# A fused attention and mixture-of-experts kernel: head 0's maxima inside the projections, merged score units masked by VectorE, token placing in the last head

## The chip, the cores and the metric

The kernel runs on one core of a Trainium2 chip. The metric is the device time of one execution in microseconds; lower is better. Three timed runs of the kernel before took 2096.61, 2099.18 and 2100.73 us, a median of 2099.18.

## The reference

Two branches read the same layer-normed input of B = 2 sequences, S = 2048 tokens, D = 512, in float32, and both are added to the input.

```python
xn = layernorm(x)                                   # [2, 2048, 512]
# attention: H = 16 heads of HD = 32, causal, with an ALiBi bias on the key position
q, k, v = (heads(xn @ W + b) for W, b in ...)
scores = einsum('bhqd,bhkd->bhqk', q, k) / sqrt(32) + slopes[h] * (key - (S - 1))
scores = where(causal, scores, finfo.min)
attn_out = softmax(scores) @ v -> merge heads -> @ Wo + bo
# experts: router on an RMS norm of xn, top 2 of E = 8, renormalised
topw, topi = top_k(softmax((norm_w * rms(xn)) @ router_w.T), 2)
a = silu(xn @ gate_w[e]) * (xn @ up_w[e]);  y = sum_e cw[e] * (a @ down_w[e]) * 4
out = x + attn_out + y
```

## The kernel before, in words

Each engine has its own in-order program; semaphores tie them. There are three stages, each a block at whose end all engines meet.

**Projections** (`project`, L200 to L700). Eight chunks of 512 tokens. A chunk has 12 PSUM tiles: four of q, four of k (by head columns) and four of v (by token rows), each the sum of 12 float32r matmuls of 512 columns (high and low parts). ACT rounds a tile (`qk_high`), DVE takes the remainder (`qk_low`), SP stores both to DRAM; v goes through DVE, ACT and POOL (`v_low`). The next chunk's input is normalised and transposed meanwhile. Router matmuls (`router_tiles`) stand at the end of a chunk, in the last chunk ahead of the v tiles. SP waits at the end until all stores have landed.

**Attention** (`attend`). 32 heads, one after another. A slot of three holds a head's `k_st` and `q_st` (rows of high and low parts, two bias rows, two rows for the query's maximum) and `v_split`. For each head there are
- M: 40 `maximum_tile` matmuls of the *next* head, up to 512 keys wide, whose row maxima DVE takes (`take_maximum`; the diagonal ones with a mask), then X (`fold_maxima`), W (`transpose_maxima`, `maxima_rows`) and a DMA that places the maxima as rows of the next head's `q_st`. The exponent then needs no subtraction;
- S: 40 score units (128 keys x up to 512 queries). On the diagonal a unit is narrower (512, 384, 256, 128 columns) and a second matmul, identity times a bf16 mask, is added (L1158). ACT takes the exponential (`weights`): unit kind P and Q twice (rounded, exact), kind W once;
- L: POOL's low part of kind P (L905); D: DVE's low part of kind Q (L981);
- V: `value_products`, two float32r matmuls for P and Q (L1170, L1172), one float32 matmul for W (L1176);
- O: ACT copies the sums, DVE adds, SP stores.

The letters of the string `ORDER` give the order in which every engine meets these (`BACK` says how many units V, L and O lag behind). `KIND` gives each unit's kind, `P_RING` the slots for probabilities. Before head 0, the attention stage loads slots 0 and 1, POOL fills the constant rows (`k_ones`, `q_ones`), DVE counts the tokens of each expert (`count_tokens`), all 40 maxima of head 0 are formed one after another, and then DVE places the tokens (`place_tokens`) ahead of its first work for head 0. The last head has no M units; in it DVE also inverts the first batch's weight sums (`first_inverses`, after the first O) and splits Wo (`split_wo`, after the second).

**Output and experts**: the output projection and 71 tiles of 128 token slots through their expert. POOL scatters the token lists first.

## Time and profile before

| | us |
|---|---|
| median of three timed runs | 2099.18 |
| the profiled execution | 2096.1 |
| its span, first to last instruction | 2094.3 |
| PE busy | 1988.7 |
| DVE, ACT, POOL busy | 1366.0, 1346.4, 1363.9 |
| granted TensorE clock, mean | 0.970 of 2.4 GHz |

Busy times are of one profiled execution. A matmul's row includes its way through the array, so consecutive rows overlap: the distance between two starts tells what one costs, not its length. "Idle before" is the engine's idle time ahead of a row and what ended it. A row that ends in x3 stands for three like it.

### The profile page before, as it was taken

The page shows a single profiled execution, that of the slowest core. Times are in us where ns is not written, and L with a number is a line of the kernel's source. Part 1 is how long each engine was busy: PE and PEld are TensorE (multiplying, and loading weights), DVE is VectorE, ACT ScalarE, POOL GpSimd, SP SyncE. Part 2 cuts the span into 40 slices and gives each one's busy share as a digit, 9 for nine tenths or more (in the row PEclk, how much of TensorE's full clock was granted, in tenths as well). Part 3 has the DMA queues.
Part 4 walks back from the last instruction along what each step waited for, and adds up shares of the span by engine and source line. Part 5 has one row for each costly group of instructions (what it writes and reads, how often), then busy time and mean ns, then how long its engine had stood idle before and what let it go on. Part 6 is the DMA issues. An engine that isn't in the chain of part 4 may idle for free. (4 is left out here: it accounts for less than half of the span.)

```text
span 2094.3 us, 40489 instructions
## 1 busy us (share of the span) xinstructions
PE 1988.7 (95%) x9182; PEld 1441.7 (69%) x9183; DVE 1366.0 (65%) x3106; ACT 1346.4 (64%) x2891; POOL 1363.9 (65%) x1262
## 2 busy tenths in 40 slices
PE   6999996799999999999999999999989989999996
PEld 4888885477777777777777777777746666666664
DVE  5454443888878888887878787888838843333332
ACT  4323321299999999999999999999972223333332
POOL 3110112188888888888989888888977625555554
PEclk9999998599999999999999999999999999999998
DMA  7577666423323232332324242323117755555554
GB/s 228 201 247 247 228 215 207 104 53 83 90 74 99 74 99 72 83 90 69 104 52 119 54 119 52 97 55 78 30 43 239 230 175 95 96 99 97 94 99 70
DMA packets 118487, 243.95 MB, mean 116 GB/s; under 512 B 15920, under 2 KB 52656, under 8 KB 112144
## 3 DMA queue, kind: packets, MB, share of 16 engines
q1 hardware_dynamic: 100464, 206.09, 33.8%
q0 software_dynamic: 17984, 37.38, 10.0%
q8 instruction: 19, 0.31, 0.1%
q14 instruction: 20, 0.16, 0.0%
HBM read 139.28 MB, written 104.21 MB: 116 GB/s over the span
## 5 line engine op out<-in xcount | busy, mean ns | idle before, releaser
L905 POOL TENSOR_TENSOR probs_lo<-probs,probs_hi 128x512 fp32r<-128x512 f32 (+2 forms) x864 | 1018.4, 1205 | 182.0 <-ACT probs L937 175.3
L936 ACT ACTIVATE probs_hi<-s_ps 128x512 fp32r<-128x512 f32 (+2 forms) x1024 | 642.5, 627 | 116.5 <-PE s_ps L1158 106.9
L937 ACT ACTIVATE probs<-s_ps 128x512 f32<-128x512 f32 (+3 forms) x1120 | 628.5, 586 | 4.7 <-PE s_ps L1155 1.1
L972 DVE TENSOR_REDUCE m_part<-m_ps 128x1 f32<-128x512 f32 x768 | 500.2, 685 | 59.3 <-PE m_ps L1137 58.0
L1155 PE MATMUL s_ps<-q_st,k_st 100*128 100x512 f32 (+1 forms) x880 | 330.2, 391 | 11.7 <-DVE probs_lo L981 5.2
L1137 PE MATMUL m_ps<-k_st,q_st 98*128 98x512 f32 (+2 forms) x880 | 325.3, 408 | 12.0 <-DVE m_part L969 6.6
L1170 PE MATMUL o_ps<-probs_hi,v_split 128*96 128x512 f32 x704 | 286.8, 407 | 0.1
L969 DVE CUSTOM_DVE_ANT_0 m_ps<-m_ps,mask_row 128x128 f32<-128x128 f32 (+3 forms) x512 | 250.8, 499 | 52.0 <-PE m_ps L1137 41.5
L1172 PE MATMUL o_ps<-probs_lo,v_split 128*96 128x512 f32 x704 | 265.9, 378 | 0.0
L1530 POOL DMA_INDIRECT out<-y,tile_rows x71 | 114.3, 1610 | 170.1 <-issue 97.9
L1155 PEld LDWEIGHTS s_ps<-q_st,k_st 100*128 100x128 f32 x880 | 168.1, 191 | 74.3 <-issue 18.0
L420 POOL TENSOR_TENSOR v_rows<-v_raw,v_rows 128x512 fp32r<-128x512 f32 x32 | 41.2, 1286 | 272.3 <-ACT v_rows L466 272.3
L1137 PEld LDWEIGHTS m_ps<-k_st,q_st 98*128 98x128 f32 x880 | 168.6, 196 | 70.7 <-DVE m_part L969 20.9
L1607 DVE SCALAR_TENSOR_TENSOR gated<-th,h_ps 128x256 f32<-128x256 f32 x71 | 29.9, 421 | 204.7 <-ACT th L1571 204.7
L1155 PE MATMUL s_ps<-q_last,k_last 100*128 100x512 f32 (+3 forms) x400 | 147.9, 385 | 0.0
L1137 PE MATMUL m_ps<-k_last,q_last 98*128 98x512 f32 (+3 forms) x400 | 143.1, 390 | 1.0 <-DVE m_part L969 0.3
L1571 ACT ACTIVATE th<-h_ps 128x256 f32<-128x256 f32 x71 | 27.3, 385 | 178.1 <-PE h_ps L1650 178.1
L981 DVE TENSOR_TENSOR probs_lo<-s_ps,probs_hi 128x512 fp32r<-128x512 f32 (+1 forms) x160 | 106.4, 665 | 53.5 <-ACT s_ps L937 52.3
L1667 PE MATMUL y_ps<-w_down,inner_t 128*128 x284 | 133.7, 593 | 0.7 <-issue 0.7
L996 DVE TENSOR_TENSOR high_sums<-o_ps,high_sums 32x512 f32<-32x512 f32 x128 | 87.7, 685 | 71.5 <-ACT high_sums L943 67.3
L1172 PEld LDWEIGHTS o_ps<-probs_lo,v_split 128*96 128x96 f32 x704 | 116.0, 165 | 21.1
L1170 PEld LDWEIGHTS o_ps<-probs_hi,v_split 128*96 128x96 f32 x704 | 118.6, 168 | 16.9 <-POOL probs_lo L905 0.7
(192 smaller groups left out, 3655.4 us busy)
## 6 DMA issues: line engine op xcount, KB each, us to landing
v_d<-v_rows SPq DMA_DIRECT2D x7, 3072.0 KB, 10.0
v_split<-v_d SPq DMA_DIRECT2D x22, 768.0 KB
k_st<-k_hi_d SPq DMA_DIRECT2D x44, 256.0 KB
q_st<-q_hi_d SPq DMA_DIRECT2D x44, 256.0 KB
xs<-in_x SPq DMA_DIRECT2D x8, 1024.0 KB, 6.8
xn_d<-xs SPq DMA_DIRECT2D x8, 1024.0 KB, 12.1
q_hi_d<-qk_hi SPq DMA_DIRECT2D x32, 256.0 KB, 7.2
q_lo_d<-qk_lo SPq DMA_DIRECT2D x32, 256.0 KB, 7.6
```

The lines of the kernel that those rows point to most:

```text
L905: nc.gpsimd.tensor_tensor(*low_operands(u), ALU.subtract).then_inc(lo_ready_pool, 1)
L936: nc.scalar.activation(probs_hi[:, u % P_RING, 0:w], scores, ACT.Exp, scale=SCALE)
L937: nc.scalar.activation(scores if KIND[u] == "Q" else probs[:, u % P_RING, 0:w], scores, ACT.Exp, scale=SCALE).then_inc(p_ready, 1)
L969: V.tensor_tensor_reduce(scores, scores, mask_row[:, M_WIDE - w:], 1.0, NEG, ALU.add, ALU.max, top).then_inc(m_taken, 1)
L972: V.tensor_reduce(top, scores, AX.X, ALU.max).then_inc(m_taken, 1)
L981: V.tensor_tensor(probs_lo[:, u % P_RING, 0:w], s_ps[:, S_BANK[u], CH - w:CH], probs_hi[:, u % P_RING, 0:w].bitcast(F32), ALU.subtract).th ...
L1137: nc.tensor.matmul(m_ps[:, m % M_BUFS, 0:w], q_st[r][0:ROW_MAX, qt * P:(qt + 1) * P], k_st[r][0:ROW_MAX, k0:k0 + w], start=True, stop=True ...
L1155: last = nc.tensor.matmul(s_ps[:, S_BANK[u], CH - w:CH], k_st[r][0:ROWS, kt * P:(kt + 1) * P], q_st[r][0:ROWS, q0:q0 + w], start=True, sto ...
L1170: nc.tensor.matmul(o_ps[0:VS, qc % 2, at], v_split[r][:, kt, :], probs_hi[:, place, 0:w], start=(kt == 0), stop=True, skip_group_check=True)
L1172: last = nc.tensor.matmul(o_ps[0:VS, qc % 2, at], v_split[r][:, kt, :], probs_lo[:, place, 0:w], start=False, stop=True, skip_group_check= ...
L1530: nc.gpsimd.indirect_dma_start(out=out, out_offset=bass.IndirectOffsetOnAxis(ap=rows[:, r:r + 1], axis=0), in_=y[:, p, :], in_offset=None, ...
L1667: last = nc.tensor.matmul(y_ps[:, p], inner_t[:, p, k], rhs, start=(k == 0), stop=(k == KF - 1))
```

## The change

1. **Head 0's maxima in the projections.** The attention buffers are allocated ahead of `project`, and the projections' own buffers are laid over others that are free then. SP issues `load_slot(0, 0)` ahead of chunk 6 (seven DMAs; it then waits for the bias store and for the ones rows) and `load_slot(1, 1)` in chunk 7 behind the first q tile's stores. POOL's memsets of the ones rows move into the projections, those of slots 1 and 2 into chunk 7. PE forms the 40 maxima within the last four tiles of chunk 6 (3, 3, 3, 2) and in chunk 7 (0, 3, 3, 3, 2, 3, 3, 3, 3, 3, 3, 0), each ahead of a group of four projection matmuls; DVE takes each tile's maxima ahead of its work on that tile. The transpose, the maxima rows and their DMA close the projections. In chunk 7 the router matmuls move ahead of the k tiles. The values of slots 0 and 1 are loaded at the start of the attention stage, with a semaphore of their own. The waits for the last stores move behind head 0.
2. **Score units merged.** Per pair of query chunks the 128- and 384-column diagonal units share a unit, and the two 256-column ones share another: 34 units instead of 40, nearly all 512 wide. A merged unit has two score matmuls, and two (W) or four (P, Q) value matmuls; exponential and low part are one instruction. Kinds go from 27 P, 8 W, 5 Q to 25 P, 5 W, 4 Q. There are new `KIND`, `ORDER` and `BACK` strings (V lags by 8), nine slots for probabilities instead of eight.
3. **The mask by VectorE.** The mask matmuls go. `mask_scores` adds the mask to the diagonal blocks in PSUM, one instruction for one or two blocks, ten a head; ACT waits for it (`s_masked`).
4. **Tokens in the last head.** `count_tokens` and `place_tokens` become one generator. In the last head DVE runs one piece of it at each of 29 turns where other heads have an M unit; the rest follows behind. ACT's exponential for the shares and PE's two counting products stand at turns 2 and 5. The expert weights' loads no longer wait for the tokens.

```diff
+    beside = ((0,) * 2 * G + (3, 3, 3, 2), (0, 3, 3, 3, 2) + (3,) * 6 + (0,))
...
+            def load_slot(n, r):
+                for p in range(QK_RING):
+                    sp.wait_ge(qk_stored[p], 32 + 32 * 2 * G // QK_RING * (NCH // B))
+                *rows, bias = slot_loads(t, n, r)
+                for dst, src in rows:
+                    sp.dma_start(dst, src).then_inc(st_loaded[r], 16)
+                sp.wait_ge(al_stored, 32)
+                sp.wait_ge(k_ones, r + 1)
+                sp.dma_start(*bias).then_inc(st_loaded[r], 16)
...
+            load_slot(0, 0)
             chunk(NCH - 2, 0, False)
             chunk(NCH - 1, 1, False, last=True)
+            sp.wait_ge(q_ones, 1)
+            sp.wait_ge(m_rows_ready, 1)
+            for dst, src in maxima_places(t, 0):
+                sp.dma_start(dst, src).then_inc(m_placed, 16)
...
+            pool.wait_ge(pj_ready, NJ * (NCH - 1) + 1)
+            for p in range(2):
+                pool.wait_ge(xn_stored[p], 16 * NCH // 2)
+            for r in range(1, HEADS_RING):
+                ones(r)
...
                 for n in range(3):
+                    for m in maxima[n:n + 1]:
+                        maximum_tile(m)
...
+        units += [whole(a, kt) for kt in range(TPC * a + 1)] + [[from_diagonal(a, 3, 0), from_diagonal(a, 1, P)], whole(b, 0)]
+        units += [[from_diagonal(a, 2, 0), from_diagonal(b, 2, CH // 2)]]
+        units += [whole(b, kt) for kt in range(1, TPC * b + 1)] + [[from_diagonal(b, 3, 0), from_diagonal(b, 1, P)]]
...
-                last = nc.tensor.matmul(s_ps[:, S_BANK[u], CH - w:CH], k_st[r][0:ROWS, kt * P:(kt + 1) * P],
-                                        q_st[r][0:ROWS, q0:q0 + w], start=True, stop=not diagonal)
-                if diagonal:
-                    last = nc.tensor.matmul(s_ps[:, S_BANK[u], CH - w:CH - w + P], ident_r, mask_s, start=False, stop=True)
+                for qc, kt, q0, w, at in S_UNITS[u]:
+                    last = nc.tensor.matmul(s_ps[:, S_BANK[u], at:at + w], k_st[r][0:ROWS, kt * P:(kt + 1) * P],
+                                            q_st[r][0:ROWS, q0:q0 + w], start=True, stop=True)
...
+            def mask_scores(n, u):
+                at = s_diagonals(u)
+                if not at:
+                    return
+                dve.wait_ge(s_ready, NS * n + u + 1)
+                if len(at) == 1:
+                    blocks = s_ps[:, S_BANK[u], at[0]:at[0] + P].unsqueeze(1)
+                else:
+                    blocks = s_ps[:, S_BANK[u], 0:2 * (at[1] - at[0])].rearrange("p (a c) -> p a c", a=2)[:, :, 0:P]
+                V.tensor_tensor(blocks, blocks, t["consts"][:, 2:3, :].to_broadcast([P, len(at), P]), ALU.add
+                                ).then_inc(s_masked, 1)
...
+                    if kind == "S":
+                        mask_scores(n, u)
...
+                    if pieces and i in FREE_TURNS:
+                        next(pieces, None)
...
+            pieces = place_tokens()
+            step_n(NH - 1, maxima=False, then=(first_inverses, split_wo), pieces=pieces)
+            for _ in pieces:
+                pass
```

## Rows read from the trace of the kernel before

**Rows 1.** The page, part 1: busy time of each engine, share, instructions.
```profile
PE 1988.7 (95%) x9182; PEld 1441.7 (69%) x9183; DVE 1366.0 (65%) x3106; ACT 1346.4 (64%) x2891; POOL 1363.9 (65%) x1262
```
**Rows 2.** Busy time by stretch: length, engines with instruction counts, clock, DMA, GB/s.
```profile
0.00:347.00 347.00, 326.45 (x1536) 269.00 (x1537) 163.48 (x487) 110.28 (x211) 59.08 (x43) 0.96 0.67 224
347.00:396.70 49.70, 23.82 (x47) 12.59 (x46) 35.51 (x90) 2.14 (x3) 10.31 (x7) 0.55 0.58 152
396.70:438.00 41.30, 35.04 (x146) 25.22 (x147) 34.44 (x87) 29.61 (x65) 27.25 (x23) 0.79 0.24 60
438.00:1521.00 1083.00, 1078.45 (x5311) 776.18 (x5309) 882.51 (x2041) 1014.65 (x2281) 951.55 (x811) 1.00 0.31 79
1521.00:1567.00 46.00, 39.99 (x170) 24.39 (x168) 18.14 (x20) 38.44 (x88) 39.64 (x32) 0.93 0.16 48
```
**Rows 3.** Transposes of maxima, one a head: ns min/median/max, first and last start.
```profile
L1142 PE MATMUL m_ps<-consts,m_max x3: 272/273/382, 392.5 to 474.1; 128*16 128x128 f32 x3
...
L1142 PE MATMUL m_ps<-consts,m_max x2: 273/273/273, 1485.0 to 1520.9; 128*16 128x128 f32 x2
```
**Rows 4.** Timeline (start, us, engine, line) and DMA issues of the seam.
```profile
344.38 5.85 SPq L354 DMA_DIRECT2D v_d<-v_rows  x2
v_d<-v_rows SPq DMA_DIRECT2D x2, 1536.0 KB, 6.3
356.88 0.36 SPq L798 DMA_DIRECT2D pairs<-in_token_pairs  x1
...
393.58 1.55 SPq L819 DMA_DIRECT2D q_st<-m_rows  x2
...
396.68 0.77 PE L1155 MATMUL s_ps<-q_st,k_st 100*128 100x512 f32 x1 [3.82 <-DMA q_st<-m_rows]
...
404.12 0.18 DVE L1070 CAST add_after<-opens 1x72 int32<-1x72 f32 x1
...
404.70 1.37 PE L1137 MATMUL m_ps<-k_st,q_st 98*128 98x512 f32 x3 [6.26 <-DVE m_part L969]
```
**Rows 5.** Timeline of PE in two places of a running head.
```profile
1517.83 1.02 PE L1176 MATMUL o_ps<-probs,v_split 128*96 128x512 f32 x2
...
1518.92 0.39 PE L1155 MATMUL s_ps<-q_st,k_st 100*128 100x512 f32 x1
...
1521.98 0.40 PE L1155 MATMUL s_ps<-q_st,k_st 100*128 100x512 f32 x1
1522.22 0.23 PE L1158 MATMUL s_ps<-mask_r 128*128 128x128 bf16 x1
1522.26 0.45 PE L1170 MATMUL o_ps<-probs_hi,v_split 128*96 128x512 f32 x1
1522.55 0.39 PE L1172 MATMUL o_ps<-probs_lo,v_split 128*96 128x512 f32 x1
```
**Rows 6.** Groups by shape, 438 to 1521 (busy us, mean ns), and ACT's timeline.
```profile
L905 POOL TENSOR_TENSOR probs_lo<-probs,probs_hi 128x512 fp32r<-128x512 f32 x631 | 802.3, 1293 | 86.5 <-ACT probs L937 80.2
L969 DVE CUSTOM_DVE_ANT_0 m_ps<-m_ps,mask_row 128x256 f32<-128x256 f32 x120 | 51.6, 430 | 4.9 <-PE m_ps L1137 0.3
L969 DVE CUSTOM_DVE_ANT_0 m_ps<-m_ps,mask_row 128x128 f32<-128x128 f32 x120 | 35.3, 294 | 8.5 <-PE m_ps L1137 6.2
...
1537.38 0.69 ACT L937 ACTIVATE probs<-s_ps 128x512 f32<-128x512 f32 x1
1537.86 0.69 ACT L936 ACTIVATE probs_hi<-s_ps 128x512 fp32r<-128x512 f32 x1
```
**Rows 7.** Timeline: POOL and DVE side by side in two places, and PE after them.
```profile
398.88 1.26 POOL L905 TENSOR_TENSOR probs_lo<-probs,probs_hi 128x512 fp32r<-128x512 f32 x1 [33.06 <-ACT probs L937]
398.96 1.23 DVE L1048 CAST idx_f<-slot_tile_i 128x64 f32<-128x64 int32 x1
...
1536.21 9.58 POOL L905 TENSOR_TENSOR probs_lo<-probs,probs_hi 128x512 fp32r<-128x512 f32 x5 [0.32 <-ACT probs L937]
...
1544.19 1.65 PE L1155 MATMUL s_ps<-q_st,k_st 100*128 100x512 f32 x3 [4.83 <-DVE probs_lo L981]
```

More of the change, by code:

```diff
@@ L124 @@
 ATTEND = attend_order()
+FREE_TURNS = [i for i, (kind, u, back) in enumerate(ATTEND) if kind == "M" and "O" in [a[0] for a in ATTEND[:i]]]
 LOOPS = (NH - 2) // HEADS_RING
@@ L137, in bank_before, with units_between @@
     return (at, 0) if at is not None else (max(v for v in range(NS) if S_BANK[v] == S_BANK[u]), 1)
+def units_between(u):
+    return next(d for d in range(1, NS + 1) if P_SLOT[(u - d) % NS] == P_SLOT[u])
+PV_START = max(units_between(u) for u in range(NS))
 VS = 3 * HD
@@ L311, in project @@
         v_low_ready = sem(ctx, "v_low_ready")
-        v_stored = [sem(ctx, f"v_stored{p}") for p in range(2)]
         al_loaded = sem(ctx, "al_loaded")
@@ L677, in _, with chunk @@
                 transpose_x(0, 0, k)
-            def chunk(c, par, ahead, last=False):
+            def chunk(c, par, ahead, last=False, first_maxima=((),) * NJ):
                 pe.wait_ge(xl_ready, 2 + KD * (c + 1))
@@ L1035, in place_tokens @@
-                step(V.tensor_tensor(starts[:, :], ends[:, :], padded[:, :], ALU.subtract))
-                step(V.tensor_tensor(base[:, :, :], so_far[:, :, :], counts[:, 1], ALU.subtract))
-                step(V.tensor_tensor(base[:, :, :], base[:, :, :], counts[:, 0], ALU.add))
-                step(V.tensor_tensor(base[:, :, :], base[:, :, :], starts[:, :].unsqueeze(1).to_broadcast([P, TT, E]), ALU.add))
+                step.issue(last)
+                yield
+                step.settle()
@@ new lines, in place_tokens @@
+                step.issue(V.tensor_tensor_scan(ends[:, :], t["ones"][:, 0:E], padded[:, :], 0.0, ALU.mult, ALU.add))
+                yield
+                step.settle()
+                step.issue(V.tensor_tensor(starts[:, :], ends[:, :], padded[:, :], ALU.subtract))
+                yield
+                step.settle()
+                step.issue(V.tensor_tensor(base[:, :, :], so_far[:, :, :], counts[:, 1], ALU.subtract))
+                yield
+                step.settle()
+                step.issue(V.tensor_tensor(base[:, :, :], base[:, :, :], counts[:, 0], ALU.add))
@@ L1039, in place_tokens @@
+                yield
+                step.settle()
+                step.issue(V.tensor_tensor(base[:, :, :], base[:, :, :], starts[:, :].unsqueeze(1).to_broadcast([P, TT, E]), ALU.add))
+                yield
+                step.settle()
                 for k in range(TOP_K):
                     last = V.tensor_tensor(hot[:, k], hot[:, k], base[:, :, :], ALU.mult)
-                step(last)
+                step.issue(last)
+                yield
+                step.settle()
                 for k in range(TOP_K):
@@ L1079, in _ @@
-            fold_maxima(0)
-            maxima_rows(0, False)
-            place_tokens()
-            def step_n(n, maxima=True, before=True, then=()):
-                for kind, u, back in ATTEND:
+                step.issue(V.tensor_scalar(after[:, :], firsts, float(P), 0.0, ALU.subtract, ALU.max))
+                yield
+                step.settle()
+                step.issue(V.tensor_tensor(opens[:, :], opens[:, :], past[:, :], ALU.max))
+                yield
+                step.settle()
@@ L1085, in step_n @@
+                yield
+                step.settle()
+                V.tensor_copy(after[:, :], opens[:, :])
+            def step_n(n, maxima=True, before=True, then=(), pieces=None):
+                for i, (kind, u, back) in enumerate(ATTEND):
                     if back and not before:
                         continue
+                    if kind == "S":
+                        mask_scores(n, u)
                     if kind == "O":
@@ L1178, in value_products @@
-                last.then_inc(pv_done, 1)
-            pe.sem_inc(pv_done, P_RING)
-            pe.wait_ge(hot_ready, 1)
-            hot2 = both[:, :, :].rearrange("p t e -> p (t e)")
-            nc.tensor.matmul(o_ps[:, 1, 0:TT * E], t["triu"], hot2, start=True, stop=True)
-            nc.tensor.matmul(o_ps[:, 1, TT * E:2 * TT * E], t["ones"], hot2, start=True, stop=True).then_inc(counted, 1)
-            pe.wait_ge(st_loaded[0], 16 * ST_DMAS)
-            pe.wait_ge(q_ones, 1)
-            for m in range(NM):
-                maximum_tile(0, 0, m, first=True)
@@ L1198, in step_n @@
                     pe.wait_ge(st_loaded[r1], 16 * ST_DMAS * st_round)
-                for kind, u, back in ATTEND:
+                for i, (kind, u, back) in enumerate(ATTEND):
+                    if not maxima and i == FREE_TURNS[5]:
+                        count_tokens()
                     if kind == "S":
```

562 lines of the change are left out of this document (343 added, 219 removed).

## Prediction

> **What bounds the kernel now.** I read the engine line of the page first: TensorE (PE) is busy 95% of the span, the other engines 64 to 65% [rows 1]. The table of busy time by stretch then splits the span [rows 2]: projections 0 to 347 us, a seam 347 to 396.7, head 0 up to its transpose of maxima at about 438, thirty heads 438 to 1521, the last head 1521 to 1567, output and experts after that. In the thirty heads PE is busy 1078.45 of 1083.00 us, ScalarE (ACT) 94%, GpSimd (POOL) 88%, VectorE (DVE) 81%: PE sets the pace, and the period is (1520.9 - 474.1)/29 = 36.10 us a head [rows 3]. In the seam PE is busy 23.8 of 49.7 us at a granted clock of 0.55. In the last head PE has 6 us without work and ACT and POOL are what runs. Nothing in the output stage is touched, so its 527 us stay.
>
> **Scale.** The profiled execution took 2096.1 us (span 2094.3), the median of the three timed runs is 2099.18. The sum is made against 2096.1, and 3.1 us are added at the end.
>
> **1. The seam.** PE's last projection ends at 347.1; the first score matmul starts at 396.68, 49.6 us later. In between lie the store of the last values (issued by 350, 6.3 us to landing), the end of the block at 356.88 when SP issues its first load, the loads of slot 0, the token counts, 40 maxima one after another and the rows' DMA [rows 4]. The change puts slot 0's and slot 1's loads and all 40 maxima of head 0 inside projection chunks 6 and 7.
> - Added to the projections: 17,408 columns of maxima. A 512-column matmul holds the next one off for 0.235 us (0.24 from 1521.98 to 1522.22 [rows 5]), so 17,408/512 x 0.235 = 8.0 us on PE, which was already 100% busy there apart from the start. DVE has room: at most three maxima and one qk_lo, 512 wide, so about 0.7 us each by the slope of [rows 6] (0.136 us per 128 columns), 2.8 us in a tile of 15 matmuls, 3.5 us.
> - Left after the projections end (call it T): values of the last tile and their low part on POOL, to T + 2.7; then SP issues the last 1.5 MB store, and behind it the two maxima rows. They are on one queue, and the store takes 6.3 us to land [rows 4], so T + 9; the rows add what they took before, 396.68 - 395.13 (last issue) = 1.6 at most and less if they only queue. I take T + 9.7 for the first score matmul. Bounds: T + 6 if the rows overtake the store (issue ends at T + 4.3), T + 14 if the block change or slot 1 is late.
> - So 49.6 - 8.0 - 9.7 = **31.9 us saved** (27 to 36).
> The added DMAs on SP's queue: seven for slot 0 ahead of chunk 6's stores, with a new wait for the bias store to land; seven for slot 1 behind chunk 7's first stores, with a wait for POOL's memsets. Together 3.1 MB. Slot 0's 1.55 MB stand ahead of chunk 6's q and k stores and delay them by about 5 us (1.5 MB land in 6.3 [rows 4]); ACT, then DVE, wait on them, but four PSUM banks of 12 x 0.235 = 2.8 us each cover 11 us, so PE sees nothing of it in my sum. With that cover gone it costs up to 5 us in each of the two chunks. The first values now load after the block change, about T + 13; DVE needs 7 us for the 11 maxima that stand ahead of the first value product, so T + 16.7 is when they are wanted.
>
> **2. Head 0.** The stretch from its first score to its transpose took 41.3 us, more than a whole period of 36.1, though no value products of an earlier head are in it. In it PE waits 6.26 us for a maximum that DVE takes only after placing the tokens [rows 4], and its granted clock is 0.79 in the mean [rows 2]. Token placing leaves this place; the clock still starts at 1.2 GHz after PE's idle stretch. I take the wait and nothing more: **6 us saved** (3 to 8).
>
> **3. The period of a head, 31 times.** Removed: 16 mask matmuls a head (bf16, 128 columns). From a 512-wide score matmul over its mask to the second product behind it are 1522.55 - 1521.98 = 0.57 us, where two 512-wide matmuls alone take 0.47: a mask costs 0.10 us [rows 5], 16 x 0.10 = 1.6 us. Score and value pieces keep their count (a merged unit still has two matmuls for scores). The kinds change: columns through the two-product form fall from 30,208 to 29,696 (-0.23 us), columns of W units rise from 2304 to 2560; a W unit of 512 costs 1518.92 - 1517.83 - 0.235 (one other matmul between them) = 0.855 us [rows 5], so +0.43. Net 1.4 us: 34.7.
> Do the others follow? ACT: 72 exponentials with 32,512 columns become 63 with 32,256. A 512-wide one follows the last by 0.48 us [rows 6], so 63 and the four copies of sums make 67 x 0.48 = 32.2 us. POOL: 27 units of mixed width become 25 of 512 at 1.293 us [rows 6], 32.3 us. DVE: busy 882.51/30 = 29.4 us a head; one 384-wide Q unit less (-0.57 by the slope); ten mask additions, four of 128 and six of 256 columns. No such addition is in the trace; the nearest rows are the masked maxima of the same widths, 0.294 and 0.430 us [rows 6], which gives 3.8 us. Its hidden bound is 0 (in DVE's idle fifth), its exposed bound is under rivals. DVE comes to 32.6 us. So all three stay under 34.7, but at 93% each where they had 81 to 94% of a longer period. For that tightness I give back 0.15 us: 34.85, a gain of 1.25 x 31 = **38.8 us saved** (0 to 50).
>
> **4. The last head.** Here the 49 small DVE instructions of counting and placing tokens arrive, in 33 pieces over 29 turns. The 39 that place took 10.9 us in the seam, from about 393.4 to 404.30 [rows 4]; at that rate all take 14, and DVE has room on paper: 18 us busy of 46 [rows 2]. But POOL is busy 39.6 of 46 there, and the rows show the two holding each other up. A cast of 64 columns took 1.23 us and ended within 0.1 us of the POOL instruction that had started just ahead of it; five 512-wide POOL subtractions took 9.58 us instead of 6.4 while DVE split Wo, and PE then waits 4.83 us for DVE [rows 7]. If each of 33 pieces waits half a POOL instruction, 0.86 x 0.65 = 0.56 us, DVE gets 14 + 18 us more, and POOL, waiting for them in turn, some 11. POOL then has about 32 + 7 + 11 = 50 us of work against a head of 46. Minus 1.5 us for ACT's shorter list, plus the masks that wait behind pieces: **6 us lost** (gain 2, loss 25).
> The Trainium skill (SBUF - State Buffer, "Who interferes with whom") says why: a VectorE instruction with two SBUF inputs, or a copy or cast in a two-port mode, and a GpSimd instruction that reads SBUF exclude each other for their whole length, while one with a single SBUF input does not. By this rule the new masks (PSUM plus one SBUF operand) are free of it and the tokens are not; a sum without it would put the last head at -1.5 us. In both places of rows 7 the trace agrees with it.
>
> **Sum.** -31.9 - 6 - 38.8 + 6 = -70.7: 2096.1 - 70.7 = 2025.4, plus 3.1: **2028 us**.
>
> **Rivals.**
> - *Tokens and POOL lock fully.* Every blockable DVE instruction, about 44, waits 0.56 us and those inside a piece a whole one: the last head grows by 25 us instead of 6. 2028 + 19 = 2047. For: the two rows of the lock. Against: pieces are spread over turns at which DVE is otherwise idle. 15%. The page of the Trainium skill named above, taken at its word for every such instruction, is this case.
> - *The masks eat what TensorE gives.* A mask stands in DVE's in-order queue behind a reduction of 0.7 us and in front of ACT. If ACT, at 93%, waits for it, the period returns to 36.1 and part 3 is lost: 2028 + 38.8 = 2067. For: DVE loses most of its slack, and ACT's own is 2.6 us a head. Against: three score banks give a unit about 2 us from its matmul to its exponential, and score, mask and handovers need about 1.5. 12%.
> - *Slower than before.* The same mask fully exposed: 0.43 for the instruction, 0.35 for the one in progress, 0.2 for two handovers, about 1 us x 10 = 10 us on ACT's 32.2, a period of 42 us, 31 x 6 = 186 us lost against 33 to 38 won at the seam: 2099 + 150 = 2249. It becomes slower than before from a period of 37.2, that is from half of the masks exposed; ACT's own list allows 2.6 us of waiting before anything is lost. 5%.
> - *The maxima are not hidden.* Stores behind slot loads stall PE in both chunks: +10, 2038, inside the range. Part of the forecast's 68%.
>
> **Numbers.** Forecast (own range 2014 to 2040) 68%, tokens 15%, masks even 12%, slower 5%. The 80% range takes in the token case and the low end of parts 1 and 3: 2010 to 2055. A measurement of this kernel tells 0.2%, some 4 us, from no change. Faster 94%, same 1%, slower 5%.
>
> **What would show it.** First score matmul at about 365 us (355 + 9.7), released by the DMA of the maxima rows; no PE wait in chunks 6 and 7; a period of 34.7 to 35.0 us between transposes of maxima; mask additions of 0.29 and 0.43 us on DVE with ACT rarely released by them; a last head of 50 to 54 us with small DVE instructions lasting over 1 us. Wrong if the period is above 35.5, if PE stands idle in the projections, or if the last head is shorter than 46.

## The result, and the profile after

The changed kernel took 2080.48 us (median of 4 runs, 2078.02 to 2083.59) where the kernel before took 2099.31 (2096.61 to 2100.73): a ratio of 0.9915, 95% interval 0.9902 to 0.9929. That is faster by 18.8 us, or 0.9%. The forecast was 2028, range 2010 to 2055: the sign was right, three quarters of the gain did not come. The profiled execution has a span of 2076.2 us.

The stretches, cut at the same events as before (end of the last projection matmul, first score matmul, transposes of maxima, first product of the output stage), from the two traces:

| stretch | before | after | change | forecast |
|---|---|---|---|---|
| projections | 347.1 | 360.8 | +13.7 | +8.0 |
| seam | 49.6 | 9.1 | -40.5 | -39.9 |
| head 0 to its transpose | 41.0 | 30.7 | -10.3 | -7.3 |
| thirty heads | 1083.2 | 1087.8 | +4.6 | -37.5 |
| last head | 49.7 | 61.4 | +11.7 | +6.0 |
| output, experts | 523.7 | 526.4 | +2.7 | 0 |

By this table the change is -18.1 us where -70.7 was forecast; 42.1 of the missing 52.6 us are in the thirty heads.

The rows behind it: the page's engine line, the busy times by stretch, and the transposes of maxima, which now run from 400.6 to 1488.4. Thirty periods between them are 36.26 us each; before it was 36.11 over the same thirty.

```profile
PE 1954.8 (94%) x8670; PEld 1418.8 (68%) x8671; DVE 1442.9 (69%) x3391; ACT 1320.5 (64%) x2603; POOL 1360.5 (66%) x1199
```
```profile
0.00:360.80 360.80, 332.27 (x1576) 275.42 (x1577) 189.40 (x544) 110.19 (x211) 69.94 (x49) 0.96 0.69 225
360.80:369.90 9.10, 0.29 (x2) 0.09 (x1) 1.41 (x4) 1.91 (x2) 1.31 (x2) 0.63 0.85 263
369.90:400.60 30.70, 30.70 (x130) 22.69 (x131) 28.46 (x70) 26.92 (x55) 25.17 (x20) 0.89 0.49 131
400.60:1488.40 1087.80, 1062.21 (x4832) 757.95 (x4831) 948.77 (x2310) 991.06 (x2011) 946.25 (x752) 1.00 0.31 79
1488.40:1549.80 61.40, 41.54 (x158) 25.81 (x157) 43.49 (x80) 39.85 (x81) 42.07 (x31) 0.90 0.13 38
...
L1374 PE MATMUL m_ps<-consts,m_max x31: 276/277/278, 400.6 to 1488.4; 128*16 128x128 f32 x31
```

In the fourth line against its partner in [rows 2] the reader sees what failed: TensorE has 479 matmuls less in thirty heads (16 masks each) and is busy 16.2 us less, but the stretch is not shorter. TensorE stands idle 25.6 us in it, where it stood 4.6 us before. It no longer sets the pace alone. (A matmul that is held back can still count as busy; the experiments below come back to this.)

The seam went as forecast. Its timeline answers to [rows 4]: the last two value stores are issued between 357.45 and 363.95, the two rows of maxima behind them from 364.06 on, and they release the first score matmul at 369.90.

```profile
357.45 6.50 SPq L454 DMA_DIRECT2D v_d<-v_rows  x2
...
364.06 3.25 SPq L510 DMA_DIRECT2D q_st<-m_rows  x2
...
369.90 0.80 PE L1385 MATMUL s_ps<-q_st,k_st 100*128 100x512 f32 x1 [7.87 <-DMA q_st<-m_rows]
```

The waits of the running heads (420 to 1500; engine, line, what it waited for, us in total, times, longest). Two are new, against none of their kind in the kernel before: ScalarE waits for VectorE's masks (the third row, 71.6 us, or 2.4 us a head), and it waits for a DMA that empties `high_sums` (the last row, 0.7 us a head). PEld is TensorE's loading of weights, which overlaps its matmuls.

```profile
POOL probs_lo L1061 <- ACT probs L1092: 140.0, 205, 1.5
PEld s_ps L1385 <- ACT probs L1092: 74.6, 176, 1.5
ACT probs_hi L1091 <- DVE s_ps L1155: 71.6, 60, 1.5
...
ACT high_sums L1098 <- DMA weight_sums_d<-high_sums: 20.2, 25, 1.4
```

The masks cost VectorE about what the forecast (0.430 and 0.294) took from the masked maxima of the same widths, 0.441 and 0.292 us (groups by shape, 400.6 to 1488.4):

```profile
L1155 DVE TENSOR_TENSOR s_ps<-s_ps,consts 128x256 f32<-128x256 f32 x180 | 79.3, 441 | 1.6
...
L1155 DVE TENSOR_TENSOR s_ps<-s_ps,consts 128x128 f32<-128x128 f32 x120 | 35.0, 292 | 0.9
```

In the last head the tokens' pieces and the split of Wo meet POOL. Timeline of 1511 to 1524: six POOL subtractions take 11.42 us, where at the running heads' 1.29 us each they would take 7.7, pieces of 8 columns take 1.2 us each, and TensorE waits 7.95 us for a low part that stands behind all of it.

```profile
1511.29 11.42 POOL L1061 TENSOR_TENSOR probs_lo<-probs,probs_hi 128x512 fp32r<-128x512 f32 x6 [1.30 <-ACT probs L1092]
```
```profile
1515.92 3.24 DVE L1351 TENSOR_TENSOR wo_lo<-wo_raw,wo_hi 128x2048 fp32r<-128x2048 f32 x1
1519.08 1.22 DVE L1219 TENSOR_SCALAR padded_i<-so_far 128x8 int32<-128x8 f32 x1
1520.34 1.18 DVE L1222 TENSOR_SCALAR padded_i<-padded_i 128x8 int32<-128x8 int32 x1
...
1523.19 0.69 DVE L1142 TENSOR_TENSOR probs_lo<-s_ps,probs_hi 128x512 fp32r<-128x512 f32 x1
```
```profile
1523.93 0.79 PE L1385 MATMUL s_ps<-q_st,k_st 100*128 100x512 f32 x1 [7.95 <-DVE probs_lo L1142]
```

### The profile page after: what moved, and what is told of

Its sections match the earlier page's. It is cut to its first block and busy times, and to the rows that moved or that the text cites. A ratio compares the mean times of both kernels' runs of the same rounds, so it can differ in the third digit from the quotient of the medians.

```text
span 2076.2 us, 38386 instructions
## 1 busy us (share of the span) xinstructions
PE 1954.8 (94%) x8670; PEld 1418.8 (68%) x8671; DVE 1442.9 (69%) x3391; ACT 1320.5 (64%) x2603; POOL 1360.5 (66%) x1199
## 3 DMA queue, kind: packets, MB, share of 16 engines
q0 software_dynamic: 17984, 37.38, 10.3%
## 5 line engine op out<-in xcount | busy, mean ns | idle before, releaser
L1061 POOL TENSOR_TENSOR probs_lo<-probs,probs_hi 128x512 fp32r<-128x512 f32 x800 | 1013.5, 1296 | 168.3 <-ACT probs L1092 168.0
L1091 ACT ACTIVATE probs_hi<-s_ps 128x512 fp32r<-128x512 f32 x928 | 597.4, 644 | 93.7 <-DVE s_ps L1155 91.2
L1092 ACT ACTIVATE probs<-s_ps 128x512 f32<-128x512 f32 x960 | 595.5, 651 | 0.2 <-DVE s_ps L1155 0.2
L1134 DVE TENSOR_REDUCE m_part<-m_ps 128x1 f32<-128x512 f32 x744 | 490.7, 684 | 11.3 <-PE m_ps L1369 5.6
L1385 PE MATMUL s_ps<-q_st,k_st 100*128 100x512 f32 (+3 forms) x880 | 323.6, 409 | 35.2 <-ACT probs L1092 17.1
L1369 PE MATMUL m_ps<-k_st,q_st 98*128 98x512 f32 (+2 forms) x840 | 281.7, 377 | 0.0
L1403 PE MATMUL o_ps<-probs_hi,v_split 128*96 128x512 f32 (+3 forms) x748 | 279.0, 383 | 1.0 <-POOL probs_lo L1061 0.5
L1404 PE MATMUL o_ps<-probs_lo,v_split 128*96 128x512 f32 (+3 forms) x748 | 269.9, 364 | 0.0
L1131 DVE CUSTOM_DVE_ANT_0 m_ps<-m_ps,mask_row 128x128 f32<-128x128 f32 x496 | 241.6, 497 | 19.2 <-PE m_ps L1369 12.8
L1404 PEld LDWEIGHTS o_ps<-probs_lo,v_split 128*96 128x96 f32 x748 | 122.9, 164 | 39.9 <-issue 6.4
L594 ACT ACTIVATE qk_hi<-pj,b_col 128x512 fp32r<-128x512 f32 x64 | 43.8, 686 | 139.4 <-PE pj L831 102.9
L1155 DVE TENSOR_TENSOR s_ps<-s_ps,consts 128x256 f32<-128x256 f32 (+1 forms) x320 | 116.2, 381 | 14.4 <-PE s_ps L1385 11.8
## 6 DMA issues: line engine op xcount, KB each, us to landing
xn_d<-xs SPq DMA_DIRECT2D x8, 1024.0 KB, 11.4
```

Source lines behind the costliest of these rows:

```text
L1061: nc.gpsimd.tensor_tensor(*low_operands(u), ALU.subtract).then_inc(lo_ready_pool, 1)
L1091: nc.scalar.activation(probs_hi[:, P_SLOT[u]], scores, ACT.Exp, scale=SCALE)
L1092: nc.scalar.activation(scores if KIND[u] == "Q" else probs[:, P_SLOT[u]], scores, ACT.Exp, scale=SCALE).then_inc(p_ready, 1)
L1131: V.tensor_tensor_reduce(scores, scores, mask_row[:, M_WIDE - w:], 1.0, NEG, ALU.add, ALU.max, top).then_inc(m_taken, 1)
L1134: V.tensor_reduce(top, scores, AX.X, ALU.max).then_inc(m_taken, 1)
L1155: V.tensor_tensor(blocks, blocks, t["consts"][:, 2:3, :].to_broadcast([P, len(at), P]), ALU.add).then_inc(s_masked, 1)
```

## The experiments

There are sixteen runs in four groups of four. "Period" is the distance of the first and last transpose of maxima in running heads, divided by 30. A ratio is against the kernel before on the same chip, with its 95% interval. The first group's chip was slower in the output stage (576 to 583 us there, at a granted clock of 0.92 to 0.93, against 522 to 528 at 0.97 elsewhere), with the kernel before at 2149.4 us. Its whole times are read only as ratios. Its periods are compared directly with those of the other groups, because the granted clock in the thirty heads is 1.00 on both chips (0.97 in e2 alone); no kernel was profiled on both. Every run that leaves the masks out has the exponent's scale at an eighth.

### Who pays for the masks?

First the masks are left out, to see whether ScalarE's 2.4 us of waiting is the loss.

```
-                if s_diagonals(u):
-                    act.wait_ge(s_masked, masked_count(n, u))
-                else:
-                    act.wait_ge(s_ready, NS * n + u + 1)
+                act.wait_ge(s_ready, NS * n + u + 1)
...
+                return          # mask_scores, VectorE
```

> The changed kernel without its masks: VectorE adds none and ScalarE waits for TensorE's score alone (the causal mask of the scores is left out, and the exponent's scale is an eighth so that nothing overflows; instructions and shapes are otherwise the same). The changed kernel has a period of 36.26 us a head where 34.85 was forecast, and in it ScalarE waits 2.4 us a head for masks. Theory A, the masks on VectorE hold the period, by the wait or by their 3.8 us of work a head: the period falls to 34.6 to 35.0, the time to 2033 to 2045. Rival B, the new order with its merged units is bound elsewhere (VectorE and ScalarE waiting for each other over the maxima and sums): the period stays at 36.0 to 36.3, the time at 2073 to 2081.

2130.66 us, ratio 0.991 (0.9894 to 0.9927); period 36.22. Theory A fell: without any mask the new order is no faster. ScalarE's idle time a head is 3.3 us, where the changed kernel had 3.2; it now waits 2.1 us for TensorE where it had waited for a mask.

```profile
L1370 PE MATMUL m_ps<-consts,m_max x31: 276/277/278, 401.5 to 1488.0; 128*16 128x128 f32 x31
```

The second run was to part ScalarE's wait from VectorE's work, with a sum of constants in the masks' place:

```
-                V.tensor_tensor(blocks, blocks, t["consts"]..., ALU.add)
+                V.tensor_tensor(masked[:, 0:w], cols, cols, ALU.add)   # w = 256 or 384
```

> The changed kernel in which VectorE, at the place of each mask, still waits for the score and then adds two stretches of a constant tile of 256 or 384 columns into a spare one (about as long as the mask it stands for), but ScalarE waits for the score alone (the mask is left out of the scores, the exponent's scale is an eighth). Tells A apart in two. A1, the wait of ScalarE for the mask is what costs: as without masks, period 34.7 to 35.1, time 2035 to 2048. A2, VectorE's added time is what costs: the period stays at 35.9 to 36.3, time 2070 to 2081. Rival B expects 36.0 to 36.3 here too, and in the run without masks.

2337.2 us, ratio 1.0853 (1.0821 to 1.0886), period (1700.7 - 412.5)/30 = 42.9. No theory had this, and the run says nothing of A1 or A2, because the stand-in was not like the mask. Both its operands and its result are in SBUF, and it took 1130 ns in the mean, where the masks, on PSUM, took 292 and 441.

```profile
L1153 DVE TENSOR_TENSOR masked<-consts 128x384 f32<-128x384 f32 (+1 forms) x320 | 361.5, 1130 | 18.7 <-PE s_ps L1382 16.1
```

Then the masks went back to TensorE, in the new order:

```
+                    if masked:
+                        last = nc.tensor.matmul(s_ps[:, S_BANK[u], at:at + P], t["ident_r"], t["mask_s"], start=False, stop=True)
```

> The changed kernel with its masks added by TensorE again, one matmul for each of the 13 diagonal blocks of 10 units (in the kernel before it was 16 blocks); merged units and order as changed. By the sum of what TensorE issues, some 34.2 us a head and 13 masks of 0.06 to 0.09: 35.0 to 35.4. Theory A: the period is 35.1 to 35.6, the time 2047 to 2062, faster than the changed kernel. Rival B: TensorE wasn't what bound it, the period stays at 36.2 to 36.6, the time at 2079 to 2092.

2168.95 us, ratio 1.0093 (1.0076 to 1.0109); period 37.27. (The expectation's "13 diagonal blocks" is miscounted: ten units hold 16.) It is worse than both theories allow. Against e1, sixteen masks cost 1.05 us a head, 0.066 each, so TensorE's work is still on the path of the new order; and with its masks where they were, the new order and its merged units are 1.16 us a head slower than the old. The fourth run is the old order with VectorE's masks:

```
+                    dve.wait_ge(s_ready, NS * n + u + 1)
+                    V.tensor_tensor(block, block, t["consts"][:, 2, :], ALU.add).then_inc(s_masked, 1)
```

> The kernel before with one edit: its 16 masks of a head are added by VectorE (at 0.29 us each, 4.6 us a head) at the place of the score in VectorE's order, and ScalarE waits for them. TensorE is rid of 16 matmuls, about 1.0 us of a period of 36.10. Theory A (a mask behind VectorE's queue holds ScalarE): 16 waits instead of 10 cost more than TensorE gives, period 37 to 39, time 2125 to 2185. Rival B (the masks are nearly free on VectorE): 35.1 to 36.0, time 2069 to 2096.

2274.19 us, ratio 1.0563 (1.053 to 1.0595); period (1640.2 - 440.8)/30 = 39.98. Here a mask behind VectorE's queue does hold ScalarE, and TensorE behind it: +4.4 us against the old order without masks (35.54, below). ScalarE waits for masks 124 us in 26 heads, 4.7 us a head (450 to 1500):

```profile
ACT probs_hi L951 <- DVE s_ps L1004: 72.8, 89, 2.4
...
ACT probs L952 <- DVE s_ps L1004: 51.2, 80, 1.1
```

So the mechanism of the forecast's rival is real. Something in the changed kernel keeps it out: its ten masks instead of 16 (the merged units), its order, or both; no run parts them.

### Where the 1.25 us went

The changed kernel was run again, for times on the chip of this group.

> The changed kernel as it is, for times on the same chip as the edits of this group. Its period was 36.26 us a head in the profile; here 36.2 to 36.3, and against the kernel before a ratio of 0.990 to 0.993, as measured.

2083.0 us, ratio 0.9926 (0.9907 to 0.9945), period 36.27.

> The kernel before without its 16 mask matmuls a head (the causal mask of the scores is left out, the exponent's scale an eighth so that nothing overflows); the order and its 40 units are as before. In its trace TensorE goes on 54 ns after each mask, 0.86 us a head, and its period is 36.10. Theory G, in the old order the masks' time comes back in full: period 35.0 to 35.3, so that the new order and units without any mask (36.22) lose about 1.1 us a head by themselves. Rival H, the old order too is held by the round with ScalarE: the period stays at 35.8 to 36.1, and nothing was to be had by taking the masks off TensorE.

2076.56 us, ratio 0.9907 (0.9886 to 0.9928); period 35.54. The period lies between the theories: of the 1.6 us that the forecast took away for 16 masks, the old order gives 0.57.

```profile
L1142 PE MATMUL m_ps<-consts,m_max x31: 272/273/273, 437.3 to 1503.4; 128*16 128x128 f32 x31
```

The two traces tell why, by the distances from one matmul's start to the next. In the kernel before, a mask has 0.054 us to the next start, 0.86 us a head, and the products of high parts take 0.53 us a head more than in e7 (7.79 and 7.26); 360 of the 480 masks in thirty heads have such a product right behind them. Together this is 1.39 us for 16 masks. Of these the period gains 0.57; the other 0.82 us come back at other matmuls: a 128-wide score now has 0.17 us to the next start, where it had 0.07. TensorE's idle time hardly shows it (5.7 us in thirty heads, 4.6 before), but its weight loads do. They now wait for ScalarE and VectorE 40.7 us where they waited 11.4, about 1 us a head more (438 to 1503; first the kernel before, then e7):

```profile
PEld s_ps L1155 <- DVE probs_lo L981: 7.0, 29, 0.2
...
PEld s_ps L1155 <- ACT probs L937: 4.4, 26, 0.2
```
```profile
PEld s_ps L1155 <- DVE probs_lo L981: 20.7, 60, 0.5
PEld s_ps L1155 <- ACT probs L937: 20.0, 69, 0.5
```

The new DMA wait was tried by moving the store that it waits for. In the changed kernel SyncE issues, each head, eight loads and then the store of the last sums (timeline of SyncE's queue):

```profile
1284.76 0.34 SPq L969 DMA_DIRECT2D k_st<-k_hi_d  x1
...
1287.78 0.35 SPq L963 DMA_DIRECT2D v_split<-v_d  x1
1288.17 0.43 SPq L981 DMA_DIRECT2D ctx_d<-high_sums  x1
1288.64 0.28 SPq L982 DMA_DIRECT2D weight_sums_d<-high_sums  x1
```

```
                 sums = 0
+                if before:
+                    store_context(n - 1, QCS - 1)
+                    sums += 1
                 if load_ahead:
...
-                    if kind == "O" and (before or not back):
+                    if kind == "O" and not back:
```

> One edit of the changed kernel: in each head SyncE issues the context and weight-sum stores of the head before (chunk 3) ahead of the eight loads for two heads on, not behind them. In the changed kernel ScalarE waits some 0.77 us a head, ending in DMA weight_sums_d, before it takes the sums of chunk 1 into the buffer that this store empties, and 1 us later TensorE waits 0.57 us for ScalarE. Theory C, this store behind the loads is one of the things that ate the gain: both waits go, the period falls to 35.5 to 35.9, the time by 10 to 22 us. Rival D, the wait is slack of the round between TensorE and ScalarE and another comes in its place: the period stays at 36.1 to 36.3.

2062.56 us, ratio 0.9834 (0.9817 to 0.9852), 20.4 us below the changed kernel on the same chip; period 35.61. Theory C holds. ScalarE's sums no longer wait for any DMA, and the waits of TensorE's weight loads for ScalarE fall from 74.6 to 47.2 us, TensorE's idle time in the thirty heads from 25.6 to 15.4:

```profile
POOL probs_lo L1064 <- ACT probs L1095: 119.3, 178, 1.4
ACT probs_hi L1094 <- DVE s_ps L1158: 72.4, 58, 1.6
PEld s_ps L1388 <- ACT probs L1095: 47.2, 123, 1.0
```

With the store out of the way, the masks were left out once more.

> The changed kernel with its stores first and without masks (the causal mask of the scores is left out, the exponent's scale an eighth). Period with stores first alone: 35.61. Theory K, the masks on VectorE are free in this order, store or no store: 35.5 to 35.65, which is the 35.54 of the old order without masks, so that order and merged units gave nothing by themselves. Rival L, their cost was only hidden under the wait for the store: 34.7 to 35.3.

2055.45 us, ratio 0.9782 (0.9758 to 0.9806); period 35.51. Theory K holds: ten masks on VectorE cost 0.10 us a head together, and the new order without them is as fast as the old order without them (35.51 and 35.54).

### What holds the rest

Five units a head (kind W) are multiplied in fp32. In the next two runs they are multiplied as two fp32r products instead, both of the rounded probabilities, so that the low part of these units is left out: first with the stores where they were, then with the stores first.

```
-                        last = nc.tensor.matmul(dst, values.bitcast(F32), probs[here], ...)
+                        nc.tensor.matmul(dst, values, probs_hi[here], ...)
+                        last = nc.tensor.matmul(dst, values, probs_hi[here], start=False, ...)
```

> The changed kernel with the five units a head that are multiplied as fp32 (kind W) multiplied instead by two fp32r products of their rounded probabilities (the products of these units are then not the reference's; ScalarE's work is the same, POOL's and VectorE's too). In the traces an fp32 unit of 512 columns is followed by 0.6 us more of TensorE than two fp32r products of 512, and the changed kernel has four of 512 and one of 384 where the kernel before had three of 512, one of 256 and four of 128. Theory E, the fp32 units are on the path and their new choice is part of the loss: the period falls by 0.8 or more, to 34.0 to 35.4. Rival F, ScalarE sets the period (it is busy 33.0 us of 36.26): what TensorE saves shows as waits of TensorE, the period stays at 35.9 to 36.3.

2064.71 us, ratio 0.9836 (0.9811 to 0.9861), period 35.64: a gain of 0.63, less than theory E's 0.8, but F is out.

> The changed kernel with its stores first and its five fp32 units a head multiplied as two fp32r products of their rounded probabilities (their products are then not the reference's). With the stores behind the loads this edit gave 0.63 us a head, and the stores first alone gave 0.66. Theory P, TensorE's own work and the holds between it and ScalarE set the period, and the two gains add: 34.8 to 35.1. Rival Q, ScalarE with 33 us of work sets it once the store is out of the way: 35.4 to 35.6.

2038.78 us, ratio 0.9714 (0.9696 to 0.9733), period (1448.8 - 404.4)/30 = 34.81. Theory P holds: the gains add (0.79 here), and TensorE's own work is on the path. Then ScalarE was relieved instead. From head 1 on, its second exponential of 26 of the 34 units covers 256 columns instead of 512, and the rest of the columns keep what an earlier unit left:

```
+                w = CH if isinstance(n, int) or KIND[u] == "Q" or S_UNITS[u][0][1] == 0 else CH // 2
```

> The changed kernel with its stores first, in which ScalarE's second exponential of 26 of the 34 units a head covers 256 columns instead of 512 from head 1 on (the rest of these columns stays what an earlier unit left there; the exponent's scale is an eighth in all units). In the kernel before such an instruction took 449 ns for 256 columns and 654 for 512, so ScalarE has some 5.3 us a head less. Rival Q, ScalarE sets the period: it falls by 2 us or more, to 31 to 33.6, or to where POOL's 31.5 us of low parts bind. Theory P, TensorE does: 34.6 to 35.5, with TensorE's waits for ScalarE (45.7 us in the loops in stores first alone) mostly gone.

2055.89 us, ratio 0.9797 (0.9781 to 0.9813), period 35.33. ScalarE is busy 4.3 us a head less (28.8 instead of 33.1), and the period falls by 0.28. The run does not clear ScalarE quite: it now waited for masks more often, 168 times in 28 heads where stores first alone had 57 in 29:

```profile
ACT probs_hi L1094 <- DVE s_ps L1159: 129.8, 168, 2.0
...
PEld s_ps L1389 <- ACT probs L1096: 17.8, 28, 0.6
```

The last run of this part moves a place in the ring of banks. The scores of 34 units go round three banks of PSUM, so twice a head a bank is taken again after two units instead of three, by units 33 and 1; here this is rotated to units 1 and 3:

```
-S_BANK = [u % S_BUFS for u in range(NS - 1)] + [1]
+S_BANK = [([v % S_BUFS for v in range(NS - 1)] + [1])[(u - 2) % NS] for u in range(NS)]
```

> The changed kernel with its stores first and the banks of the scores rotated by two units: 34 units go round 3 banks, so one bank is taken again after two units instead of three, twice a head; as it stands unit 33 waits for unit 31's exponentials there (TensorE stands 0.64 us in every head before its first product), rotated it is units 1 and 3. Theory R, this stand is on the path: it goes and nothing of its size takes its place, the period falls to 34.9 to 35.3. Rival S, ScalarE was busy then, and its next wait for TensorE (1.3 us before unit 1) grows or TensorE waits one unit on: 35.5 to 35.8.

2087.5 us, ratio 0.9946 (0.9929 to 0.9963), period (1498.6 - 405.3)/30 = 36.44. Both theories were wrong: TensorE's idle time at the old place shrank by only 0.27 us (0.48 to 0.21), and 7 us later, before unit 3, it loses 0.83 us. The old place of the short distance was the better one.

### Last head and first stage

All four runs of this part have their stores first and are read against e5. In the last head the split of Wo was moved behind the last sum:

```
-            step_n(NH - 1, maxima=False, then=(first_inverses, split_wo), pieces=pieces)
+            step_n(NH - 1, maxima=False, then=(first_inverses,), pieces=pieces)
...
             add_sums(NH - 1, QCS - 1)
+            split_wo()
```

> The changed kernel with its stores first (the edit of the run before) and a second edit: in the last head VectorE splits Wo (spread_r, wo_hi, wo_lo, some 6 us, with POOL's product beside it stretched from 7.7 to 11.4 us over six) after its last piece of the tokens and the last sum, not between them after chunk 0. From the last head's transposing row to the first product of the output stage it is 62.1 us with stores first alone, 49.7 in the kernel before. Theory I, the split in the middle holds ScalarE and TensorE behind VectorE (waits of 7.3 and 7.9 us): 54 to 58 us, the whole 3 to 8 us less than stores first alone. Rival J, the pieces themselves are the price, or the split now is late for the output: 61 to 65 us, no gain or a loss of up to 3 us.

2057.63 us, ratio 0.981 (0.9794 to 0.9827). The stretch is 57.6 us instead of 62.1; the last value product comes 51.6 us after the transpose instead of 58.1. Theory I holds. Alone, the split takes VectorE 3.9 us instead of 6.2:

```profile
1526.09 0.40 DVE L1349 CAST spread_r<-spread_raw 64x512 fp32r<-64x512 f32 x1
1526.60 1.23 DVE L1352 CAST wo_hi<-wo_raw 128x2048 fp32r<-128x2048 f32 x1
1527.86 2.29 DVE L1354 TENSOR_TENSOR wo_lo<-wo_raw,wo_hi 128x2048 fp32r<-128x2048 f32 x1
```

Then all token pieces were put behind the head, with the split left in its middle:

```
-            step_n(NH - 1, share_at=FREE_TURNS[2])
+            step_n(NH - 1)
             take_sums(NH - 1, QCS - 1)
+            share_weights()
```

> The changed kernel with its stores first, and all of the assignment of tokens (VectorE's pieces, ScalarE's share, TensorE's count) after the last head's work instead of in its free turns; the split of Wo stays where it was. Theory J, the pieces in the free turns are the price of the last head: its heads' work ends 8 to 12 us earlier than in stores first alone, but the tokens then stand alone behind it, some 15 to 20 us of short VectorE instructions, so the last stretch is 65 to 72 us and the whole 3 to 10 us slower. Theory I, the split of Wo is the price: the last head's own work ends no more than 4 us earlier, the last stretch is 72 to 80 us, the whole 10 to 18 us slower.

2064.79 us, ratio 0.9841 (0.9825 to 0.9858). The last value product comes at 48.3 us (9.8 sooner), the output stage at 64.7 (2.6 later). So the pieces cost 9.8 us in the head and the split 6.5, not independently. Put behind the head, the pieces lengthen the way from the last product to the output stage from 4.0 to 16.4 us, 12.4 more, so by the profiled runs the free turns are still their better place; the whole times (0.9841 and 0.9834) don't tell the two apart.

In the first stage the loads of slot 0 were issued inside chunk 6:

```
-            load_slot(0, 0)
-            chunk(NCH - 2, 0, False)
+            chunk(NCH - 2, 0, False, slot=True)      # load_slot(0, 0) after the stores of g == G
```

> The changed kernel with its stores first, and SyncE issues the loads of slot 0 after the fifth tile's stores of the projections' chunk 6 instead of ahead of the chunk. In the traces ScalarE waits up to 7.2 us there for a store of q (DMA q_lo_d) that stands behind these loads, and TensorE waits 2.8 to 4.9 us for VectorE's x_lo that comes of it; the projections ended 13.7 to 21 us later than in the kernel before, where 8.0 were forecast. Theory M, the loads ahead of the chunk's stores make this wait: it goes or falls under 1 us, the projections end 3 to 7 us sooner than with stores first alone (367.7). Rival N, the loads are only moved to where they delay other stores, or come late for the first maxima: no change within 1.5 us, or up to 5 us later.

2063.35 us, ratio 0.9839 (0.982 to 0.9859); the projections end at 361.5, within the 360.2 to 368.1 that this point takes over the changed kernel and its edits. The wait for x_lo (2.8 us in the changed kernel, 1.6 to 4.9 in the others) is gone, and another has its place, as rival N had it. Slot 0's loads now come late for the first maxima:

```profile
PE mp L816 <- DMA k_st<-bias_d: 4.2, 1, 4.2
```

> The changed kernel with its stores first, the split of Wo after the last head's sums, and the loads of slot 0 issued after the third tile's stores of chunk 6 (neither ahead of the chunk, where TensorE then waited 2.8 to 4.9 us for VectorE's x_lo, nor after the fifth's, where it waited 4.2 us for DMA k_st from bias_d instead). Theory M, this place is between the two waits: the projections end at 356 to 360 and the whole is 3 to 6 us below the run with stores first and late split (2057.6). Rival N: either wait comes back in another size, 361 to 365, the whole within 2 us of it.

2055.31 us, ratio 0.9792 (0.9772 to 0.9812); projections to 364.9, and the wait for the bias row is 3.0 us. Rival N holds. Against e8's ratio of 0.981 this is no measurable step. With stores first and the late split, it has the lowest time of the kernels here that leave nothing of the computation out: 2.1% below the kernel before, 1.2% below the changed one by the ratios (0.9792/0.9915).

## Why the prediction was wrong, point by point

- **Part 1: the seam right, its price in the projections too small.** The first score came at T + 9.1 where T + 9.7 was said, released by the maxima rows. The 8.0 us added to the projections were 13.7 in the profiled run, and more in others (364.5 in after_again against 347.7 in e7, the old order on the same chip: 16.8). So the part saved 26.8 us where 31.9 were said. The forecast said that four banks of PSUM would cover the stores behind slot 0's loads. They did not: ScalarE waited 7.2 us for a store of q (DMA q_lo_d) behind the loads (4.6 at the longest before, when TensorE did not wait), VectorE 6.98 for ScalarE, and TensorE 2.8 us for x_lo in chunk 6; two waits of 0.9 us for maxima came on top. e11 and e14 show that this wait comes from the place of the loads, and that each other place tried has a wait of its own. The maxima rival (+10) was right in mechanism, at a little over half its size (5.7).
- **Part 2, head 0: right, a little small.** The stretch took 30.7 us, 10.3 less, where 6 and 1.25 were said. TensorE's wait of 6.3 us is gone (it is busy 30.70 of 30.70 us), as forecast. The rest came with 16 matmuls fewer and a granted clock of 0.89 instead of 0.79, for which the forecast took nothing; no run parts the two.
- **Part 3, the period: wrong; this is the step that failed.** The forecast was 34.85, the period 36.26. The runs give one chain of steps to it:

```
36.11  kernel before
-0.57  its 16 masks left out (e7): 35.54; the forecast took 1.6
-0.03  new order, merged units, new kinds, stores first, no masks (e10): 35.51; the forecast took +0.20
+0.10  ten masks on VectorE (e5): 35.61; the forecast took +0.15 for tightness
+0.66  the last sums' store behind eight loads (after_again): 36.27; not in the forecast
```

  The chain depends on its order: in the new order, stores behind the loads, the same 16 masks on TensorE are worth 1.05 us and not 0.57 (e1, e3). No run has the new order with stores first and masks on TensorE, so how much is the mask's price and how much the order's is not settled between the two.

  Two steps of the forecast failed. First, a mask's 0.10 us was read at one place and multiplied by 16, as if TensorE's time came back whole. Over thirty heads 16 masks took 1.39 us, 0.087 each, so the price was a little high; the greater error is that only 0.57 of it came back, because TensorE then waits for ScalarE and VectorE (e7). "Busy 99.6%" said that TensorE was hardly ever seen idle. It did not say how far away the next wait was. Second, the forecast followed the changed instructions of four engines but not the new distance between a store that did not change and its reader: in one late head the store of weight_sums_d is issued 16.3 us after the transpose (15.1 before), and the sums that need its buffer are wanted at 22.8 us (in the same head of e5; 25.95 before): 6.5 us between them where there had been 10.8, and ScalarE stood until 23.8. The question "Do the others follow?" was asked of the engines' busy time alone. That busy time itself was forecast well: ScalarE 33.0, VectorE 31.6 and GpSimd 31.5 us a head, where 32.2, 32.6 and 32.3 were said.
- **The rival "masks eat what TensorE gives" (2067, 12%)** named a period of 36.1, and 36.26 came, but its cause is refuted for this order (e1, e10). What made it look true, ScalarE's 71.6 us of waiting for masks, was time in which it would have waited for TensorE (59.7 us of such waits in e1). That the number of this rival came out near the measured period is luck. In the old order it is true and costs 4.4 us a head (e4).
- **Part 4, the last head: mechanism right, size too small.** +11.7 where +6 was said. The lock of VectorE and POOL was seen; that the split of Wo would stand in the middle of a locked stretch, with pieces of 1.2 us and a low part behind it, was not priced: 4.5 us (e8). The rest is the pieces. The page of the Trainium skill that the prediction cites ("SBUF - State Buffer", "Who interferes with whom") agrees again with rows here: the same difference of two SBUF tiles took 3.24 us beside POOL and 2.29 alone, and pieces of 8 columns took 1.2 us beside POOL where a cast of 64 columns (at 1530.28) took 0.20 between its instructions, while the masks with PSUM operands kept 292 and 441 ns. The prediction's largest tokens rival (+25 instead of +6) was further off than its forecast.
- **"Nothing in the output stage is touched":** 526.4 against 523.7; over all runs on such chips 521.9 to 528.0, so this is within the spread.
- **What stays open.** Which order would win the 0.8 us that the old order's masks leave as waits: e12, e13 and e15 show that TensorE, ScalarE and the place of the short bank distance each bear on the period (0.79 for the fp32 units, 0.28 for 4.3 us of ScalarE, 0.83 for the banks the wrong way), none with all of it. Why the new order costs 1.16 us more than the old when TensorE keeps the masks (e3) was not taken apart; the store behind the loads, worth 0.66 with VectorE's masks and 0.71 without any (e1, e10), is probably the larger part of it.

## What to carry to other kernels

An engine at 99% busy bounds a kernel only down to the next wait: before 1.6 us of its work are counted as won, take that work out alone and see what the period gives (here 0.57). When an order is rewritten, check the distance between every buffer's emptying DMA and its next writer, too, and what is issued ahead of that DMA on its queue; here putting one store before eight loads was worth 20.4 us (e5), more than the whole change (18.8). A large wait on a new instruction is a loss only if the engine would not have waited there for another.

## What was not expected of the hardware

A sum of 256 or 384 columns with all operands in SBUF took VectorE 1.13 us in the mean beside POOL's stream of 128x512 subtractions, which went from 1.29 to 1.36 us. In the last head of the changed kernel a sum of 256 columns of the same kind took 0.40 us while POOL was idle (at 1524.52) and 1.52 beside it (at 1526.49). So 3.8 us of planned work became 11.3 us a head (361.5 us over 32 heads) and the period 42.9. The same engine's mask additions on PSUM, with the same POOL beside them, kept their 0.29 and 0.44 us. And 16 bf16 mask matmuls of 128 columns, with 54 ns in the mean from a mask's start to the next matmul's, were worth 36 ns each when taken out of one order (e7) and 66 ns when put into the other (e3).
